# Second half's first context scan as two TensorE products per chunk, in a fused decay-scan and butterfly-FFN kernel

## What is computed

```
ln(x)  = (x - mean) / sqrt(var + 1e-5)
r[s]   = 0.9 * r[s-1] + ctx[s]*ctx[s]          # along the tokens of a batch
x      = x + ln(x) * r
h      = ln(x) @ W_exp + b_exp                 # 512 -> 2048
h      = butterfly(h, up_weights)              # 11 stages of 2x2 mixing over 2048
h      = gelu(h + up_bias)
h      = butterfly(h, down_weights)
out    = x + h @ W_con + b_con + down_bias     # 2048 -> 512
```

## Time and profile before

| what | value |
|---|---|
| three executions, median (us) | 2779.53 |
| the profiled execution, its own time (us) | 2781.72 |
| its span, first to last instruction (us) | 2779.9 |
| TensorE busy | 2737.4 us, 98% |
| VectorE, ScalarE, GpSimd busy | 77%, 41%, 15% |
| mean granted TensorE clock | 0.992 |
| DMA | 542.57 MB, mean 195 GB/s |

### The profile page before, as it was taken

How to read it: one execution, slowest core, us unless ns; L and a number is a source line. 1 busy time by engine, 2 the same in 40 slices (tenths; PEclk the granted TensorE clock), 3 DMA queues, 4 the chain that set the end, 5 groups by cost and what they waited for, 6 DMA issues and landing times.

```text
span 2779.9 us, 34990 instructions
## 1 busy us (share of the span) xinstructions
PE 2737.4 (98%) x12141; PEld 2255.1 (81%) x12141; DVE 2127.0 (77%) x3562; ACT 1138.0 (41%) x1705; POOL 406.2 (15%) x577
## 2 busy tenths in 40 slices
PE   8789999999999999999999999999999999999999
PEld 6668888888888888888888888888888888888887
DVE  8968787787878778787877878777787877788533
ACT  5843434334343443434344343433434343343432
POOL 4721011010101102010110201111020111101000
PEclk8999999999999999999999999999999999999999
DMA  9885665758567585856748575675847657585543
GB/s 265 282 288 161 195 201 170 224 152 244 162 198 209 165 228 153 232 173 190 214 159 237 152 226 181 178 222 160 239 152 219 189 171 225 164 239 152 182 151 99
DMA packets 294709, 542.57 MB, mean 195 GB/s; under 512 B 37430, under 2 KB 101078, under 8 KB 277638
## 3 DMA queue, kind: packets, MB, share of 16 engines
q1 hardware_dynamic: 287632, 536.82, 64.5%
q0 software_dynamic: 1488, 2.27, 0.4%
q10 hardware_dynamic: 5414, 1.25, 0.3%
HBM read 445.83 MB, written 60.82 MB: 182 GB/s over the span
## 4 chain that ended last, share of the span: by engine, by line
PE 94%; DVE 1%; DMA 1%; SPq 0%; ACT 0%; issue 0%; POOL 0%; DVEq 0%; ACTq 0%
PE ps L1682 44%; PE ps L1700 25%; PE ps L1713 25%; DMA w1r<-w_products 0%; PE ps L1762 0%; SPq L554 0%; DVE xop L1138 0%; SPq L496 0%; DVE x L1195 0%; DVE w1r L1138 0%; POOL raw L489 0%; DVE raw L1242 0%; DMA raw<-kv 0%; DVE raw L1192 0%; DVE kv L1222 0%
## 5 line engine op out<-in xcount | busy, mean ns | idle before, releaser
L1682 PE MATMUL ps<-xop,w1r 128*128 128x512 f32 x5376 | 1365.3, 390 | 9.5 <-DMA w1r<-w_products 6.9
L1682 PEld LDWEIGHTS ps<-xop,w1r 128*128 128x128 f32 x5376 | 1010.1, 188 | 220.5 <-DMA w1r<-w_products 7.3
L1700 PE MATMUL ps<-w2r,ghi 128*128 128x512 f32 x2048 | 630.5, 389 | 0.0
L1713 PE MATMUL ps<-w2r,ghi 128*128 128x512 f32 x2032 | 626.7, 390 | 0.0
L957 ACT ACTIVATE st<-ps 128x512 f32<-128x512 f32 x384 | 229.6, 598 | 851.0 <-PE ps L1682 851.0
L1332 DVE TENSOR_TENSOR x<-ps,x 128x512 f32<-128x512 f32 x508 | 348.5, 686 | 282.9 <-PE ps L1713 280.4
L1700 PEld LDWEIGHTS ps<-w2r,ghi 128*128 128x128 f32 x2048 | 384.4, 188 | 79.8
L1713 PEld LDWEIGHTS ps<-w2r,ghi 128*128 128x128 f32 x2032 | 381.8, 188 | 80.0 <-DVE glo L1355 0.4
L1350 DVE TENSOR_TENSOR g<-ps,st 128x512 f32<-128x512 f32 x384 | 262.6, 684 | 223.1 <-PE ps L1682 223.1
L961 ACT ACTIVATE g<-g,gelu_bias 128x512 f32<-128x512 f32 x384 | 275.5, 718 | 363.9 <-DVE g L1350 363.9
L1355 DVE TENSOR_TENSOR glo<-g,ghi 128x512 fp32r<-128x512 f32 x510 | 346.4, 700 | 79.4 <-ACT ghi L975 79.3
(11 more groups left out here) (166 smaller groups left out, 1706.6 us busy)
## 6 DMA issues: line engine op xcount, KB each, us to landing
w1r<-w_products SPq DMA_DIRECT2D x889, 256.0 KB, 3.3
w2r<-w_split SPq DMA_DIRECT2D x126, 1024.0 KB, 5.0
x<-in_x_dram SPq DMA_DIRECT2D x128, 256.0 KB, 7.1
raw<-kv SPq DMA_DIRECT2D x496, 64.0 KB, 2.2
out_dram<-x SPq DMA_DIRECT2D x120, 256.0 KB, 4.0
kv<-in_ctx_dram SPq DMA_DIRECT2D x64, 256.0 KB, 7.5
raw<-in_ctx_dram SPq DMA_DIRECT2D x64, 256.0 KB, 5.2
w_split<-w2s SPq DMA_DIRECT2D x10, 512.0 KB, 6.7
```

The lines of the kernel that those rows point to most:

```text
L1682: last = nc.tensor.matmul(bank[:, :], w1r[:, slot, w, c * P:(c + 1) * P], xop[:, XPOS[m], v, c, :], start=(opens and i == 0), stop=(i == l ...
L1700: last = nc.tensor.matmul(ps_ya[j][:, :], g[:, p % 2, q, j * P:(j + 1) * P], w2r[:, p % 2, kk, w, :], start=(p == 0 and kk == 0 and i == 0 ...
L1713: last = nc.tensor.matmul(ps_yb[:, :], g[:, p % 2, q, j * P:(j + 1) * P], w2r[:, p % 2, kk, w, :], start=(kk == 0 and i == 0), stop=(kk == ...
```

## The change

1. `step_matrices()` on VectorE, ahead of `scan_chunk(0, 0, 0)`, makes two 128 by 128 matrices from `ident` by short scans: `step_rows` (powers of 0.9 inside a chunk) and `carry_rows` (the carry from the last token of the chunk before).
2. `scan_chunk(1, 1, j)` is gone. TensorE's `scan_step(j)` takes its place: two fp32 products with 512 columns into PSUM bank j. The second needs the chunk before in SBUF: ScalarE copies it (`keep_step`, and `carried_rows` for the end of half 0). Steps 0 to 2 follow `high_up` 13, 14 and 15, step 3 follows `turn_high` 1. Step 0 waits for `low_matrix_ready` 2, which is `top_products(1)` on VectorE. `gate(1, 1, j)` reads the bank. `save_carry(1)` makes the carry for the next tile.
3. The bias transpose and the bias product move ahead of `high_up`, around `spread_low_dn`, into bank 3. ScalarE copies their results before it makes `HX[:, 0]`.
4. `spread_high_dn` moves from ahead of `high_up` to one stage behind each of `high_up` 4 to 7, so `spread_low_dn(PARTED)` now comes first.
5. All moves of half 0 go to SyncE, behind a wait for `step_made` 1.
6. VectorE evicts `back` for odd k; its `gate`, `weights_lo` and `normalise` calls are in a new order. ScalarE's `weights_hi(0)` is parted around `turn_high`.

```diff
-        FOLD += [("back", k, "act") for k in range(KH)]
+        FOLD += [("back", k, "dve" if k % 2 else "act") for k in range(KH)]
...
             sp.wait_ge(xn_turned, J)
+            sp.wait_ge(step_made, 1)
             move_xT(sp, 0, 0, xT_moved[0])
             move_xT(sp, 0, 1, xT_moved[0])
+            move_xT(sp, 0, 2, first_moved[0])
+            move_xT(sp, 0, 3, first_moved[0])
...
             weight_sums(0)
+            rstd_gated(1, (0, 1))
             weight_sums(1)
-            first_moves(0)
+            rstd_gated(1, (2, 3))
             weight_sums(2)
...
+            def keep_step(j):
+                act.wait_ge(step_made, j + 1)
+                act.activation(ctx_rows_of(1)[:, j, :], ps[j][:, :], ACT.Copy).then_inc(step_kept, 1)
...
+            act.wait_ge(gate_turned, J)
+            act.activation(carried_rows, ctx_rows_of(0)[:, J - 1, :], ACT.Copy).then_inc(step_kept, 1)
+            act.wait_ge(bcol_turned, 1)
+            act.activation(bcol, ps[BIAS_BANK][:, 256:256 + 2 * KH], ACT.Copy).then_inc(bcol_kept, 1)
             top_hi(1)
...
+            act.wait_ge(bias_low, 1)
+            act.activation(yb, ps[BIAS_BANK][:, 256:256 + KH], ACT.Copy).then_inc(yb_kept, 1)
             act.wait_ge(path_product, UP_DONE)
...
-            for q in range(R // 4):
+                if r >= R - 3:
+                    keep_step(r - R + 3)
+            weights_hi(0, (0, 1))
+            for q in range(2):
                 fold_step("turn_high", q)
-            weights_hi(0)
+            keep_step(3)
+            for q in range(2, R // 4):
+                fold_step("turn_high", q)
+            weights_hi(0, (2,))
...
+            def step_matrices():
+                nc.vector.tensor_tensor_scan(out=step_rows[:, :], data0=decay[:, 0:P], data1=ident[:, :], initial=0.0,
+                                             op0=ALU.mult, op1=ALU.add).then_inc(steps_ready, 1)
+                nc.vector.memset(carry_rows[:, :], 0.0).then_inc(carry_picked, 1)
+                dve.wait_ge(carry_picked, 1)
+                nc.vector.tensor_scalar(carry_rows[:, 0:P:Q], ident[:, Q - 1:P:Q], DECAY, None, ALU.mult)\
+                    .then_inc(carry_picked, 1)
+                dve.wait_ge(carry_picked, 2)
+                nc.vector.tensor_tensor_scan(out=carry_rows[:, :], data0=decay[:, 0:P], data1=carry_rows[:, :], initial=0.0,
+                                             op0=ALU.mult, op1=ALU.add).then_inc(steps_ready, 1)
...
             top_products(1)
-            scan_chunk(1, 1, 0)
-            scan_chunk(1, 1, 1)
-            scan_chunk(1, 1, 2)
+            gate(1, 1, xs[0], 0)
+            gate(1, 1, xs[0], 1)
+            gate(1, 1, xs[0], 2)
+            save_carry(1)
+            gate(1, 1, xs[0], 3)
             weights_lo(0)
             weights_lo(1)
-            scan_chunk(1, 1, 3)
-            gate(1, 1, xs[0], 0)
             weights_lo(2)
-            gate(1, 1, xs[0], 1)
-            gate(1, 1, xs[0], 2)
-            weights_lo(3)
-            gate(1, 1, xs[0], 3)
-            weights_lo(4)
             normalise(0, 1, xs[0], 0, first=True)
             normalise(0, 1, xs[0], 1, first=True)
-            weights_lo(5)
+            weights_lo(3)
             normalise(0, 1, xs[0], 2, first=True)
             normalise(0, 1, xs[0], 3, first=True)
+            weights_lo(4)
+            for k in range(4):
+                fold_step("back", k)
+            weights_lo(5)
...
+            def scan_step(j):
+                if j == 0:
+                    pe.wait_ge(low_matrix_ready, 2)
+                    pe.wait_ge(steps_ready, 2)
+                    pe.wait_ge(squared, 2)
+                rows = ctx_rows_of(1)
+                nc.tensor.matmul(ps[j][:, :], step_rows[:, :], rows[:, j, :], start=True, stop=False)
+                pe.wait_ge(step_kept, j + 1)
+                nc.tensor.matmul(ps[j][:, :], carry_rows[:, :], rows[:, j - 1, :] if j else carried_rows,
+                                 start=False, stop=True).then_inc(step_made, 1)
...
             spread_high(range(HIGH))
+            pe.wait_ge(path_product, LOWS)
+            pe.wait_ge(bias_loaded, 4 * NX)
+            nc.tensor.transpose(ps[BIAS_BANK][:, 256:256 + 2 * KH], bias_rows, ident[0:2 * KH, 0:2 * KH])\
+                .then_inc(bcol_turned, 1)
             spread_low_dn(range(PARTED[0]))
-            spread_high_dn(range(HIGH))
+            pe.wait_ge(bcol_kept, 1)
+            for k in range(KH):
+                last = nc.tensor.matmul(ps[BIAS_BANK][:, 256 + k:257 + k], LX[:, 0, k, :], bcol[:, k:k + 1],
+                                        start=True, stop=True)
+            last.then_inc(bias_low, 1)
             pe.wait_ge(high_matrix_ready, 1)
             for r in range(R):
...
                 if r == 3:
+                    pe.wait_ge(yb_kept, 1)
                     spread_low_dn(PARTED)
+                if 4 <= r < 4 + HIGH:
+                    spread_high_dn((r - 4,))
...
+                if r >= R - 3:
+                    scan_step(r - R + 3)
             pe.wait_ge(high_matrix_ready, 2)
-            for q in range(R // 4):
+            for q in range(2):
                 fold_step("turn_high", q)
...
+            scan_step(3)
+            for q in range(2, R // 4):
+                fold_step("turn_high", q)
```

More of the change, by code:

```diff
@@ L154, in xattn_ffn_program @@
         gelu_bias = sb("gelu_bias", [P, KH])
+        step_rows = sb("step_rows", [P, P])
+        carry_rows = sb("carry_rows", [P, P])
+        assert STEPS_PER_BATCH > 1
         hc_up = scr[:, 0:HIGH * PAIRS * 4].rearrange("p (s m e) -> p s m e", s=HIGH, m=PAIRS)
@@ L250, in xattn_ffn_program @@
         gate_turned = sem("gate_turned")
+        steps_ready = sem("steps_ready")
+        carry_picked = sem("carry_picked")
+        step_made = sem("step_made")
+        step_kept = sem("step_kept")
         stats1_done = sem("stats1_done")
@@ L346, in spreads, with chunk @@
             return dn * (LOWS + HIGH) + stage + 1
-        SPREAD_ORDER = (list(range(LOWS + HIGH)), [*range(PARTED[0]), *range(LOWS, LOWS + HIGH), *PARTED])
-        def spread_count(dn, stage):
-            return dn * (LOWS + HIGH) + SPREAD_ORDER[dn].index(stage) + 1
+        BIAS_BANK = 3
+        carried_rows = raw[:, 0, 0, :]
+        def chunk(t, j):
+            return t * J + j - (J if t > 1 else 0)
         UP_DONE = LOWS + HIGH
@@ L525, in _ @@
             wcon_src = w_con.rearrange("(k e r) d -> (k e) (r d)", e=E, r=R)
-            sp.wait_ge(coef_spread, spread_count(1, LOWS - 1))
+            sp.wait_ge(coef_spread, spreads(1, LOWS - 1))
             for part in range(2):
@@ L1064, in path_products @@
                     bank, col = places[stage]
-                    dve.wait_ge(coef_spread, spread_count(dn, first + max(stage, PARTED[0] - 1)))
+                    dve.wait_ge(coef_spread, spreads(dn, first + max(stage, PARTED[0] - 1)))
                     if prev is None:
@@ L1143, in scan_chunk @@
             def scan_chunk(t, h, j):
-                n = t * J + j
+                n = chunk(t, j)
                 rows = ctx_rows_of(h)[:, j, :]
@@ L1167, in scan_chunk, with save_carry @@
                 nc.vector.transpose(rows, flat).then_inc(gate_turned, 1)
+            def step_matrices():
[8 more added lines that the diff above has]
+                                             op0=ALU.mult, op1=ALU.add).then_inc(steps_ready, 1)
+            def save_carry(t):
+                dve.wait_ge(step_kept, J + 1)
+                dve.wait_ge(xn_turned, t * J)
+                nc.vector.transpose(kvT[:, :, :].rearrange("p b i -> p (b i)"), ctx_rows_of(1)[:, J - 1, :])\
+                    .then_inc(carry_picked, 1)
+                dve.wait_ge(carry_picked, 3)
+                nc.vector.tensor_scalar(carry[:, :].bitcast(i32), kvT[:, :, Q - 1].bitcast(i32),
+                                        keep[:, bass.ds(t, 1)], None, ALU.bitwise_and).then_inc(carry_picked, 1)
+                dve.wait_ge(carry_picked, 4)
             def means1(t):
@@ L1189, in gate @@
                     dve.wait_ge(rstd1_ready, t + 1)
-                    dve.wait_ge(gate_turned, t * J + J)
+                    if t != 1:
+                        dve.wait_ge(gate_turned, chunk(t, J))
                     dve.wait_ge(mean1_ready, t * J + J)
-                nc.vector.scalar_tensor_tensor(out=rows, in0=x[:, c, :], scalar=mv1[:, j, 0:1], in1=rows,
+                if t == 0 and j == J - 1:
+                    dve.wait_ge(step_kept, 1)
+                scan = rows
+                if t == 1:
+                    dve.wait_ge(step_kept, j + 2)
+                    dve.wait_ge(step_made, min(j + 2, J))
+                    scan = ps[j][:, :]
+                nc.vector.scalar_tensor_tensor(out=rows, in0=x[:, c, :], scalar=mv1[:, j, 0:1], in1=scan,
                                                op0=ALU.subtract, op1=ALU.mult).then_inc(gated, 1)
@@ L1262, in _ @@
             dve.wait_ge(bias_row_ready, 1)
```

(23 more changed lines are left out.)

16 lines of the change are left out of this document (removed).

## The result

The changed kernel takes 2793.76 us (median of five executions, 2792.33 to 2795.63) beside 2779.67 for the kernel before on the same chip (2779.27 to 2780.95). The ratio is 1.0047, with a 95% interval of 1.0036 to 1.0059: 14.1 us slower, where 9.0 were forecast (2788.5). The direction and the wide range (2777 to 2796) held; the size did not, since the forecast's own range ended at 2791.5. The time is that of rival C (2793.5). The profiled execution took 2795.63, its span is 2793.8, 13.9 over the one before.

The account below looks back on a forecast made before the run. TensorE bound 94% of the span, its unbroken stretch starting by fold end and SyncE's queue. High fold 7.4 late, plus 8.4 to `high_dn` (15.8), then 14.3, 10.9, 10.6, finally 9: span 2788.9, forecast 2788.5 us, range 2777 to 2796.

Parts of the forecast that it names:

- rival C: Fold's end: ScalarE's 14.3 passes through, alternating `back` evictions make it wait, DMA queue stays full; 14 later, 2793.5; chance 0.13.
- Bias product ahead, 7.2 at half clock: Ahead of the high fold near 52: 32 records at 1.2 GHz take 7.2 us, with 3.6 as the other end.
- rival A's first way: Bias product runs at full clock, 3.6 less; one way of rival A (part absorbed, middle 2783), whose whole chance is 0.22.
- High fold 7.4 late, HX without its cover: Start of `high_up`: `HX[:, 0]` is made only after the bias product, so TensorE waits; 64.2 against 56.76.
- The scan step's place and `high_dn`, 15.8 late: TensorE's scan waits for `low_matrix_ready` at 87.9; scan, fold and `turn_high` steps put first `high_dn` at 100.0 against 84.23.
- VectorE's saving is lost: VectorE in the fold: net 7.5 less work, but about 11 us of waiting for the two spreads.
- rival B: Fold: VectorE was the bound and ScalarE has slack, so the net 7.5 come off, 2772; chance 0.13.
- its 37.1 of 40.5: ScalarE's busy time before the change, from 84.2 to 124.74, where its first token operation begins: 37.1 of 40.5 us.
- SyncE and the end of the fold: Half 1 moves at 134.9 against 124.30 put the first load 10 later; this later path decides, less 1.
- a relief of 1: SyncE's queue, emptier at its start, gives back 1 of the 10 us delay of the first load.
- the fold's own end: Other path: first token operation near 139, `low_dn` 22, products begin at 162, used up at 176, 5 late.
- The saving of 2.4: In `low_dn` at the fold's end: 22 needed instead of 24.4, because the moved tokens are there.

Follow-up runs that it names:

- e10: Changed kernel with the bias product's 32 single-column records issued twice (64): 2800.09 us, ratio 1.0069.
- e1: Changed kernel with ScalarE copying `yb` behind the HX activations, which then don't wait for the bias product: 2789.76 us, ratio 1.0034.
- e8: Kernel before with item 3 alone: bias product ahead of the high fold, `spread_high_dn` between it and `high_up`: 2785.71 us, ratio 1.0019.
- e7: Changed kernel with all `back` on ScalarE, half 1 moves ahead of `store_w1(5)`, `spread_high_dn` ahead of `high_up`, bias product at `high_up` 13: 2783.17 us, ratio 1.0008.
- e9: e7 with scan steps behind `high_dn` 1, 3, 5 and 7, and `weights_lo(0)` and (1) ahead of the gates reading them: 2783.55 us, ratio 1.0010.
- e4: Changed kernel with all sixteen `back` evictions on ScalarE again: 2793.45 us, ratio 1.0048.
- e11: Kernel before with item 4 alone: `spread_high_dn` one stage behind each of `high_up` 4 to 7: 2783.53 us, ratio 1.0009.
- e5: e4 with SyncE's moves of half 1 ahead of `store_w1(5)` instead of behind it: 2788.71 us, ratio 1.0032.
- e2: Changed kernel with `spread_high_dn` back ahead of `high_up`, behind the bias product: 2786.36 us, ratio 1.0021.
- e3: Changed kernel with the bias transpose at `high_up` 10 and the bias product at `high_up` 13: 2790.24 us, ratio 1.0035.
- e6: e5 with `spread_high_dn` also back ahead of `high_up`, as in e2: 2784.30 us, ratio 1.0012.

## Why the prediction was right, and where its size failed

**Bias product ahead, 7.2 at half clock: right.** 6.98 measured, clock 0.50 there. The windows of the changed kernel (columns as in the earlier trace rows) show the level in its three places: under the product, in the idle time behind it, and with the first `high_up`:

```profile
52.00:56.00 4.00, 4.00 (x20) 3.94 (x19) 3.82 (x8) 0.00 (x0) 1.51 (x2) 0.50 1.00 368
59.00:63.00 4.00, 0.05 (x1) 0.00 (x0) 3.84 (x12) 3.91 (x9) 3.07 (x4) 0.50 1.08 276
64.00:66.00 2.00, 2.00 (x11) 2.00 (x11) 0.42 (x1) 0.36 (x1) 0.65 (x1) 0.50 1.31 130
```

e10 settles what stood open in the prediction: twice as many records run 13.8 us without a pause and stay at 1.2 GHz, 0.216 us each, and the time rises by 5.1. So rival A's first way falls. The Trainium skill (TensorE: Matmul & The Clock Gate, Part 1) says that sustained activity releases the throttle. With the second half at full clock the 64 records would have taken 3.4 us less, an estimate from the 3.63 us of 32 such records. The trace does not agree for these products with a single column.

**High fold 7.4 late, HX without its cover: right.** Measured 6.8. e1 shows that 3.5 of it, the wait of HX for the product, cost 4.8 at the end (4.4 by the traces), and e8 that item 3 alone costs 5.3 in a kernel whose VectorE still scans.

**The scan step's place and `high_dn`, 15.8 late: right within 1.4.** From 88.15 to 98.65 TensorE does the eight products, two `high_up` and four `turn_high` steps (in the timeline four groups of eight records), 10.5 us or 0.87 for each of the twelve groups, where 7.8 + 1.8 + 2.2 = 11.8 were taken: the four scan steps are 7.0 instead of 7.8, the six fold steps 3.5 instead of 4.0.

**VectorE's saving is lost: right.** It waits 5.0, 7.1 and 4.8. (The terms of the saving give 7.7 where the prediction has 7.5; nothing hangs on it.) Even with items 3 and 4 and the shared `back` taken off (e7) the difference to the kernel before is +2.7, with an interval of -0.3 to +4.7, so rival B falls in every version run: the scans that left VectorE gave nothing back. That ScalarE bounds the fold, and that it hangs on `high_dn`, was argued from its 37.1 of 40.5; e9 starts `high_dn` 4.7 earlier without a gain, so it isn't that alone. What the fold's middle is bound by once `high_dn` is early stays open: VectorE waited 11.0 for ScalarE and TensorE 6.2 for ScalarE, but no run gave ScalarE less to do there.

**SyncE and the end of the fold: this step failed, by size.** The prediction compared two paths, SyncE's queue (10 late, 9 after a relief of 1) and the fold's own end (products at 162, used up at 176, 5 late). It overlooked that the two meet earlier. The w1 loads stand in SyncE's queue behind the stores of the last splits, so a late fold holds the loads too, and not only TensorE's first products. Its own numbers gave that already: 139 + 22 = 161 for the last split is 11.7 late. Measured it is 16.6. In the trace after, SyncE had done the stores of `w1r` at 158.03 (154.12 + 3.91; 11.3 late, near the 10.6 forecast for its path) and then stood 4.7 us waiting for ScalarE's split:

```profile
154.12 3.91 SPq L554 DMA_DIRECT2D w_products<-w1r  x3
162.72 4.73 SPq L562 DMA_DIRECT2D w_split<-w2s  x4
```

The chain of the changed kernel, in order of time, goes the same way:

```profile
137.86 0.61 DVE wcon L1155
138.52 1.97 PE ps L1650 x8
...
165.20 0.61 DVE w2s L1151
165.83 0.32 SPq L562
...
174.65 9.49 DMA w1r<-w_products
```

From the last split to the stretch there are three terms, and they add up to the loss:

| us | before | after | e4 |
|---|---|---|---|
| last split on SyncE | 149.27 | 165.83 | 161.19 |
| from there to the load's issue | 10.10 | 8.82 | 10.36 |
| its landing, to the stretch | 11.19 | 9.53 | 10.96 |
| stretch | 170.56 | 184.18 | 182.51 |

+16.6 - 1.3 - 1.7 = +13.6. The relief of a queue that has emptied was taken as 1 and is 2.9; the delay in front of it was taken as 10 and is 16.6. Of the 16.6, 13.9 were there at `weights_hi(5)` (14.3 forecast). 1.5 came in `back`: ScalarE had fewer evictions, but now waited for TensorE, which waited for VectorE's evictions, which stood behind `weights_lo`. This is rival C's mechanism, in ScalarE's and VectorE's waits (total us, times, longest):

```profile
ACT wcon L839 <- PE ps L1650: 5.8, 4, 2.8
```

```profile
DVE wcon L1155 <- PE ps L1650: 3.8, 4, 1.5
```

The last 1.1 came in `low_dn`: from the first token operation to the last split it took 25.7, where 24.5 were before and 22 were forecast. The saving of 2.4 was argued from the moved tokens being there. The wait for them is gone (the chain of before has one, the one of after none), and the stage got no shorter:

```profile
128.40 3.38 DMA raw<-kv
```

In the chain of after the stage is turns between TensorE and ScalarE, part of it at a lower clock:

```profile
156.00:160.00 4.00, 4.00 (x7) 1.44 (x5) 2.13 (x3) 1.91 (x5) 3.64 (x3) 0.62 1.02 400
```

In e4, where the granted clock was 1.00 from 142 to 160, the same stage took 23.4 (137.82 to 161.19). So the 25.7 hold some 2 us that e4 did not have; whether they are the clock's or the order's no run separates.

So rival C had the size right and half of the reason: everything passed through, and `back` had its part (1.5 in the fold's end here, 2.3 at the first token operation and 4.6 at the last split in e4). But without it, in e4, only 1.1 us come back: from the last split to the stretch it takes 21.3 again, as in the kernel before, since SyncE's queue is right behind. In the changed kernel "the DMA queue is as full as ever" was wrong, it was 2.9 emptier. Step by step, the forecast's 179.6 for the stretch becomes 181.3 if the paths meet at the last split (161 + 21.3 - 1), 185.0 with 25.7 for `low_dn` instead of 22, 186.1 with the first token operation at 140.16, and 184.2 with a relief of 2.9 instead of 1. The stage that was mis-sized is thus the larger of the two errors, and the relief hid a part of them.

How the 14.1 divide: alone in the kernel before, item 3 costs 5.3 (e8) and item 4 2.7 (e11). Going from the changed kernel to e7 step by step, taking off the shared `back` gives 1.1 (e4), SyncE's new order then 4.7 (e5), taking off items 3 and 4 together 5.5 (e5 to e7), and 2.7 are left, with the scan on TensorE and the half clock under its first step. The 4.7 are a gain of an order that the kernel before doesn't have, and so not the price of a part of the change. These parts overlap (e2 takes off item 4 alone and gains 8.2, since `spread_high_dn` fills the gap that item 3 makes), so none is the price of its item in every order.

## What to carry to other kernels

Before two paths are compared by their ends, follow each queue backwards to the first place where an instruction of one path stands behind one of the other; the later of the two decides there, and not at the end. Work that is taken off an engine with the longest run of work is worth at most what the next engine in the chain can start earlier, so look first at what the replacement is queued ahead of: here eight products of 0.87 us stood ahead of everything that ScalarE waited for. (That is needed and not enough: e9 moved them away and gained nothing.) And an operation that costs nothing under a cover costs its full time when it is moved to where there is none, as `spread_high_dn` and HX did when the one that covered the other was moved.

## What the runs showed of the hardware

- In these runs products of a single column did not bring TensorE's clock back: 64 of them, issued without a pause for 13.8 us, stayed at 1.2 GHz (e10). Where they began at full clock, the clock fell behind them: in e7 they ran at 2.4 GHz (32 in 3.63), and the granted clock is 1.00 under them and 0.50 right behind; before and e3 show the same.

```profile
75.50:78.90 3.40, 3.40 (x34) 3.40 (x32) 1.30 (x3) 1.16 (x2) 2.75 (x1) 1.00 0.43 178
79.00:82.00 3.00, 3.00 (x5) 1.30 (x5) 0.00 (x0) 0.18 (x1) 0.00 (x0) 0.50 0.00 0
```

- The time that an issue takes on SyncE is not fixed: the eight moves of half 1 took it 8.78 us (1.10 each) in the changed kernel and 9.49 in e4, where they follow a store without a pause, 6.83 in e5, where they do so too, and 5.95 (0.74 each) before, where 2.3 us lie between. What sets it stays open: e9's eight took 9.26 at a DMA share of 0.92, e7's 6.81 at 0.96.
- The versions e5, e6, e7 and e9 spread more from one execution to the next than the kernel before: 5.5 to 8.6 us from lowest to highest, against 4.1 in the 28 executions of the kernel before beside the first three and 5.2 in the 21 beside e9. Nothing here tells why.
